# Weighting the rows of two chunks at once in an attention pass of a four-layer graph network

## The reference

```python
h = (x @ W.T).reshape(n, H, D)
h_src = h[src]
...
alpha = jnp.where(alpha >= 0, alpha, 0.2 * alpha)
amax = jax.ops.segment_max(alpha, dst, num_segments=n)
ex = jnp.exp(alpha - amax[dst])
denom = jax.ops.segment_sum(ex, dst, num_segments=n)
attn = ex / jnp.maximum(denom[dst], 1e-10)
out = jax.ops.segment_sum(h_src * attn[..., None], dst, num_segments=n)
```

## Time and profile before

| | us |
|---|---|
| median of 3 runs | 8846.99 (8846.64 to 8849.97) |
| profiled execution | 8844.68 |
| its span | 8842.9 |
| second pass of the attention, first multiply to the end of the last add | 7024.5 to 7634.0 |
| VectorE busy over the span | 5795.6 (66%) |
| TensorE matmuls busy over the span | 5516.0 (62%) |

### The profile page before, as it was taken

The page is one execution under the profiler, slowest core; times in us unless marked ns, Lnnn a source line. Parts: engine busy times, 40 slices in busy tenths (PEclk is TensorE's granted clock), DMA queues, the critical chain, the costliest instruction groups (busy, mean ns, idle before and its releaser), DMA issues. The chain is left out here.

```text
span 8842.9 us, 98679 instructions
## 1 busy us (share of the span) xinstructions
PE 5516.0 (62%) x21277; PEld 3079.4 (35%) x21277; DVE 5795.6 (66%) x15735; ACT 2945.2 (33%) x9436; POOL 5601.3 (63%) x5671
## 2 busy tenths in 40 slices
PE   2224980000677777777767777756767789687775
PEld 1113770000444444444532222343333333333332
DVE  8999980000777775555559999877777799833333
ACT  0000220000566652222238888733333366300000
POOL 5777777776777766777537777527777300077775
PEclk9999775555788888888869999977666699866665
DMA  2001320001555554555548888628888555333334
GB/s 94 6 6 40 117 86 11 3 3 38 158 166 159 160 143 148 166 161 166 151 120 242 242 242 242 175 80 243 244 243 243 136 175 176 102 105 105 105 105 87
DMA packets 796177, 1192.24 MB, mean 135 GB/s; under 512 B 161213, under 2 KB 631923, under 8 KB 788941
## 3 DMA queue, kind: packets, MB, share of 16 engines
q0 software_dynamic: 259712, 606.96, 26.1%
q1 hardware_dynamic: 535885, 578.95, 20.5%
HBM read 926.73 MB, written 258.64 MB: 134 GB/s over the span
## 5 line engine op out<-in xcount | busy, mean ns | idle before, releaser
L1178 POOL DMA_INDIRECT ring<-scaled_table,idx_s x832 | 787.3, 946 | 1024.9 <-DVEq L193 771.8
L1405 POOL DMA_INDIRECT big<-y_table,idx_s x832 | 859.5, 1033 | 480.3 <-issue 246.3
L1794 POOL DMA_INDIRECT ring<-att_table,rec_d_sb x808 | 778.9, 964 | 458.6 <-DVEq L193 206.4
L1473 PE MATMUL bank<-big,wts 128*128 128x512 f32 x1664 | 831.9, 623 | 364.0 <-DVE big L1397 364.0
L334 POOL DMA_INDIRECT rec_s<-acc,big x784 | 836.4, 1067 | 322.4 <-issue 256.5
L1034 POOL DMA_INDIRECT big<-x_table,rec_d_sb x808 | 812.2, 1005 | 300.5 <-issue 227.3
L2147 PE MATMUL bank<-ring,acc 128*128 128x256 f32 x1664 | 829.8, 621 | 239.3 <-DMA ring<-scaled_table,idx_s 202.3
L1178 POOL DMA_INDIRECT ring<-h_table,rec_d_sb x808 | 765.0, 947 | 310.7 <-issue 201.7
L334 POOL DMA_INDIRECT rec_d<-x_res,big x784 | 750.6, 957 | 255.7 <-issue 255.7
L1813 PE MATMUL bank<-big 128*128 x2424 | 594.4, 373 | 273.0 <-DVE acc L1904 219.0
L1215 PE MATMUL bank<-ring,acc 128*128 128x256 f32 x1616 | 549.0, 466 | 225.4 <-DMA ring<-h_table,rec_d_sb 222.6
(11 more groups left out here) (348 smaller groups left out, 12643.2 us busy)
## 6 DMA issues: line engine op xcount, KB each, us to landing
weights_dram<-big SPq DMA_DIRECT2D x104, 1024.0 KB
big<-weights_dram SPq DMA_DIRECT2D x832, 128.0 KB, 3.5
rows_spill<-ring SPq DMA_DIRECT2D x808, 128.0 KB
big<-rows_spill SPq DMA_DIRECT2D x808, 128.0 KB, 2.2
ring<-key_dram SPq DMA_DIRECT2D x49, 1024.0 KB
big<-dl_dram SPq DMA_DIRECT2D x50, 512.0 KB
big<-y_table,idx_s POOLq DMA_INDIRECT x832, 4.0
ring<-scaled_table,idx_s POOLq DMA_INDIRECT x832, 2.8
```

The source lines that it names most:

```text
L1178: g.indirect_dma_start(out=slot[:, c % ring_len, :], out_offset=None, in_=table, in_offset=bass.IndirectOffsetOnAxis(ap=index(c), axis=0)) ...
L1405: g.indirect_dma_start(out=yg[:, n % RY, :], out_offset=None, in_=y_table, in_offset=bass.IndirectOffsetOnAxis(ap=idx_s[:, n:n + 1], axis= ...
L1473: pe.matmul(ps[4 + u % 4], oh1[c // 4 % 2][:, c % 4, :], mid[:, c % (2 * RM), 0:512], start=(c % 2 == 0), stop=(c % 2 == 1)).then_inc(summ ...
L1794: g.indirect_dma_start(out=ag[:, n % R3, :], out_offset=None, in_=att_table, in_offset=bass.IndirectOffsetOnAxis(ap=recd3i[:, n, D_IDX:D_I ...
```

## The change

`weighted_rows` now multiplies chunks c and c + 1 in one VectorE operation with 2 x 256 elements per partition, for even c only. It waits for both landings and for `summed` of one chunk more. `msgs_v` counts pairs: TensorE waits for the pair of its chunk, and SyncE, before it loads into a buffer, for the pair of the chunk that lay there. The adds are as before, one for each chunk in steps 4 and on; the rest of the pass is unchanged.

```diff
             for c in range(NCD):
                 if c >= RB:
-                    sp.wait_ge(msgs_v.s, msgs_v.n(c - RB + 1))
+                    sp.wait_ge(msgs_v.s, msgs_v.n((c - RB) // 2 + 1))
                 sp.dma_start(hs[:, c % RB, :], rows_spill[c]).then_inc(spill.s(c, RB), 16)
 
         def weighted_rows(eng, c):
             eng.wait_ge(exps.s, exps.n(c // 4 + 1))
-            eng.wait_ge(spill.s(c, RB), spill.n(c, RB))
+            for k in (c, c + 1):
+                eng.wait_ge(spill.s(k, RB), spill.n(k, RB))
             if c >= 8:
-                eng.wait_ge(summed.s, summed.n(c - 7))
-            return eng.tensor_tensor(msg[:, c % 8, 0:D].rearrange("p (h d) -> p h d", h=H),
-                                     hs[:, c % RB, :].rearrange("p (h d) -> p h d", h=H),
-                                     lanes(msg[:, c % 8, D:TW], H, HD), ALU.mult)
+                eng.wait_ge(summed.s, summed.n(c - 6))
+            both_msgs, both_rows = msg[:, c % 8:c % 8 + 2, :], hs[:, c % RB:c % RB + 2, :]
+            return eng.tensor_tensor(both_msgs[:, :, 0:D].rearrange("p c (h d) -> p c h d", h=H),
+                                     both_rows.rearrange("p c (h d) -> p c h d", h=H),
+                                     both_msgs[:, :, D:TW].rearrange("p c (h o) -> p c h o", o=1)
+                                     .to_broadcast([P, 2, H, HD]), ALU.mult)
...
-                pe.wait_ge(msgs_v.s, msgs_v.n(c + 1))
+                pe.wait_ge(msgs_v.s, msgs_v.n(c // 2 + 1))
...
-                if c < NCD:
+                if c < NCD and c % 2 == 0:
                     weighted_rows(v, c).then_inc(msgs_v.s, 1)
```

## The result

| | before | after | difference |
|---|---|---|---|
| median, 11 runs each | 8849.62 | 8927.45 | +77.8 us |
| ratio, 95% interval | | | 1.0089 (1.0080 to 1.0097) |
| profiled execution | 8844.68 | 8924.08 | +79.4 |
| second pass, first multiply to end of last add | 609.5 | 690.9 | +81.5 |
| the rest of the profiled execution | | | -2.1 |

The account below looks back on a forecast made before the run. VectorE was taken to set the second pass's pace, 0.675 us a chunk. Pairs +97.0, loads -13.4, start and end +0.3, odd steps -1 sum to +83 us: 8930 us from the median, range 8912 to 8955.

Parts of the forecast that it names:

- A pair of chunks: VectorE in the second pass: 1.592 us a pair in place of 1.35, +97.0 us from first to 804th add.
- the multiply's additional waits: Double multiply waits for two landings and one more chunk of TensorE; none late, costed at nothing.
- The double multiply: One 512-element multiply: 685 ns shown, 0.602 us to next start; 0.07 us a pair gained, 28 us in 404 pairs.
- The second add's wait: Second of two neighbouring adds waits for the first to complete: 0.65 us in place of 0.34, 404 times.
- The loads: Block-number loads every 16 chunks on VectorE's sequencer: stall 0.84 us in place of 1.105, -13.4 us in 50.
- Start and end: Second pass: three double multiplies before the first add instead of five single, +0.3 us; tail of four adds unchanged.
- Odd steps: About 6 us of irregular steps in the pass may partly vanish into new idle time: -6 to 0, taken as -1.
- Sum: All terms of the second pass together: +83 us, 8928 from the profiled execution, 8930 from the median.
- The rule of the Trainium skill: Next operation starts only when the pipe is empty, waits cost nothing extra; rival 1 by it: 8786 us, chance 0.03.
- Rival 2: New idle time drops TensorE's clock for good in the pass, 0.88 us a chunk: +105 us, 8952; chance 0.06.

Follow-up runs that it names:

- The order alone: Kernel before, single multiplies kept, VectorE's order changed to multiply, multiply, add, add: ratio 1.0113 to the kernel before, pass 715.3 us.
- four adds in a row: Changed kernel with four chunks in one multiply (1024 elements), then four adds: 8945.64 us against 8835.56 of the kernel before, ratio 1.0123.
- the removal of the wait: Changed kernel with adds of odd chunks in a second accumulator, each add waiting only for the one before the last: ratio 0.9931 to the kernel before.

## Why the prediction was right, point by point

- *A pair of chunks.* Forecast 0.65 + 0.34 + 0.602 = 1.592; measured 0.644 + 0.346 + 0.602 = 1.592. The two small errors cancel. The 0.006 us more between add and multiply, some 2.5 us in all, are not the multiply's additional waits: single multiplies behind two adjacent adds have 0.347 too, and double multiplies with two accumulators have 0.339. They go with the wait between the adds. Costing the additional waits at nothing was right.
- *The double multiply.* Forecast 685 ns shown and 0.602 to the next start; 685 and 0.602. Its worth, put at 28 us, was 24.3 with the wait and 33 without (loads included in both).
- *The second add's wait.* It was taken from four adds at the end of the pass, at 0.65; 0.644 in the loop. The order alone, four adds in a row and the removal of the wait show it as the cause. Of the 402 gaps of 0.22, the profile names the add before for at most 338 and TensorE for most of the others, where the prediction had the add before for all.
- *The loads.* Forecast a stall of 0.84 in place of 1.105; the measured stretch over a load is 1.784, less 0.942: 0.84. That it is the load, not TensorE, was argued from the timeline and is shown by the runs with the load first and with two accumulators, in which TensorE's part is unchanged.
- *Start and end.* First add 3.34 us behind the first multiply in place of 3.07: +0.27, forecast +0.3. Odd steps: 684.6 us from the first to the 804th add, less 639.0 and 50 x 0.84, is 3.6 in place of 6.1; -2.5, forecast -1.
- *Sum.* The pass +81.5 where +83 was forecast; the profiled execution +79.4, as the stages ahead of the pass were 1.9 us shorter, which no part of the change explains. The median, 8927.45, is 2.5 us below the forecast of 8930; that it is so close is in part luck, as single executions of the changed kernel lie between 8921 and 8935.
- *The rule of the Trainium skill* (page "VectorE: DVE Perf Modes", section "The DRAIN you can't avoid") that a wait costs nothing extra does not hold here: adds with the wait start 0.65 us apart, adds without it 0.34, in kernels that differ in that. The prediction left out a sentence of the same section of the Trainium skill, that an operation which nothing holds back starts earlier; the 0.34 us agree with that one. Its advice to reduce the number of operations (same page, section "Rules for kernel authors") is good for 24 to 33 us by itself, not for the estimate of 63 from the page's formula, since operations without a wait overlap. The formula's 691 ns for one operation of 512 elements is near the 685 measured.
- *Rival 2, the lower clock.* Half of its condition came true and none of its price: the clock fell, but only for short spells. This table of windows (us, busy time of PE, PEld, DVE, ACT and POOL with counts, granted clock, DMA share, GB/s) has the whole pass, a spell at the lower clock and what follows it:

```profile
7022.00:7714.00 692.00, 483.86 (x1616) 299.10 (x1616) 561.22 (x1214) 400.35 (x1185) 0.00 (x0) 0.94 0.52 151
7110.30:7113.50 3.20, 3.20 (x9) 1.99 (x7) 2.71 (x6) 1.49 (x6) 0.00 (x0) 0.50 0.58 159
7113.70:7123.80 10.10, 6.59 (x25) 3.88 (x24) 8.09 (x18) 6.42 (x19) 0.00 (x0) 1.00 0.54 158
```

The granted clock is 0.94 over the pass, where it was 1.00: it falls to 0.50, 1.2 GHz, in 21 short spells. In the one shown TensorE is busy throughout; just before it TensorE had been idle for 1.30 us at a load of block numbers, and such an idle time (1.3 to 1.7 us) ends within 0.6 us of the start of each of the 21. It stands at the other loads too, without a fall. The prediction had argued from 1.3 us of idle time in the kernel before; that holds for the load of the earlier trace rows, but over the 50 loads it was 1.10 in the median, where now it is 1.30. VectorE does not notice:

```profile
7109.20 0.68 DVE L1981 TENSOR_TENSOR ring<-big,ring 128x512 f32<-128x512 f32 x1
...
7110.79 0.69 DVE L1981 TENSOR_TENSOR ring<-big,ring 128x512 f32<-128x512 f32 x1
...
7112.59 0.69 DVE L1981 TENSOR_TENSOR ring<-big,ring 128x512 f32<-128x512 f32 x1
```

The first distance is 1.59 us, and the second, in the spell, 1.80, of which 0.20 more than usual lies between add and multiply (7112.04 to 7112.59 in place of 0.35). Such steps come 12 times in the pass, and only this one falls in a spell; another is 7303.88 to 7304.43, in a long stretch with a granted clock of 1.00. So the clock is not their cause; what it is stays open, and all of them make 2.6 us. Leaving out those with a load, the 63 pairs that touch a spell take 1.592 us in the median, as the 288 others do. The reason given for harmlessness, that TensorE falls behind by 0.17 us a pair and has about two us of slack, agrees with this; the slack itself was not measured.

## What to carry to other kernels

When operations are merged, look at what becomes a neighbour. A chain of operations that wait for each other costs no pace as long as something independent and long enough lies between any two links (here 0.675 us against the 0.65 that the wait asks for), and merging the independent ones takes that away. Here 404 merges saved 0.07 us each and 402 waits of 0.31 us each were laid bare. If the chain is made into two (an accumulator for even and one for odd), the same merge pays, and together with the early load of register values the pass went from 609.5 to 524.5 us, with 7.0 us behind it for joining the accumulators. An idle time that the profile gives to another engine should be compared with what the waiting engine's own sequencer does at that moment.

## What the runs showed of the hardware

- From start to next start, VectorE's multiplies of 256, 512 and 1024 elements took 0.335, 0.602 and 1.136 us, where they are shown as 418, 685 and 1219 ns long. An add of 264 elements took 0.34 us with no wait for it, and 0.64 to 0.65 where the next add waited for it.
- VectorE's sequencer began a load up to three operations ahead of the add that needed it when no open wait stood in front of the load. A load of 16 registers, 1.10 us long, cost 1.105 us in the order of before, 0.84 with a double multiply to cover it, 0.51 with double multiplies and two accumulators, and 0.05 with the load first besides.
- The granted clock of TensorE fell to 0.50 in 21 short spells of the changed kernel, though TensorE was busy 0.70 of the time (483.86 of 692 us), each at the end of an idle time of 1.3 to 1.7 us. In the kernel before, with 545.82 of 612 us busy and idle times of 1.10 us at most loads (1.46 the longest), it did not fall once the pass had started up. The spells cost nothing here: VectorE sets the pace, and the pairs in a spell took the same 1.592 us as the others.
